# Attention on one Trainium2 core: query turned whole in pairs of heads, its high and low parts written into opposite halves of the partitions

## The reference

```
xn = layernorm(x) * g_norm
q  = xn @ Wq            # 16 heads of 64
k, v = xn @ Wkv         # one head of 64, shared by all query heads
q, k = l2norm(q) * q_scale, l2norm(k) * k_scale
p  = softmax(8 * q @ [null_k, k].T + bias)   # bias: rel_pos_bias with a causal mask, and the mask input
o  = p @ [null_v, v]
out = layernorm(o @ Wout) * g_out
```

## Time and profile before

| | us |
|---|---|
| median of 3 runs | 2564.28 |
| lowest and highest | 2559.71, 2566.23 |
| profiled execution, span | 2563.2 |
| TensorE busy, matmul | 2394.0 (93%) |
| VectorE busy | 1753.9 (68%) |
| GpSimd busy | 1333.1 (52%) |
| ScalarE busy | 1234.0 (48%) |

### The profile page before, as it was taken

The page is one execution under the profiler, slowest core; times in us unless marked ns, Lnnn a source line. Parts: engine busy times, 40 slices in busy tenths (PEclk is TensorE's granted clock), DMA queues, the critical chain, the costliest instruction groups (busy, mean ns, idle before and its releaser), DMA issues. The chain is left out here.

```text
span 2563.2 us, 56453 instructions
## 1 busy us (share of the span) xinstructions
PE 2394.0 (93%) x20705; PEld 1977.5 (77%) x20705; DVE 1753.9 (68%) x4121; ACT 1234.0 (48%) x3133; POOL 1333.1 (52%) x1464
## 2 busy tenths in 40 slices
PE   5999999999999999977999999988899999999998
PEld 3788888888888888845777777766677877778776
DVE  4576767677767676677888888337865755746764
ACT  3656666666666666554555555114333333332332
POOL 3676767676767676535666666215422322322332
PEclk8999999999999999988999999999999999999999
DMA  4000100000000000001122221216022112111211
GB/s 143 7 11 9 46 18 11 10 10 9 11 10 9 10 5 5 5 15 24 40 56 55 55 53 47 55 59 181 32 66 63 55 58 67 58 47 62 66 34 59
DMA packets 156689, 105.05 MB, mean 41 GB/s; under 512 B 85168, under 2 KB 134832, under 8 KB 156416
## 3 DMA queue, kind: packets, MB, share of 16 engines
q1 hardware_dynamic: 130928, 62.69, 9.0%
q10 hardware_dynamic: 25488, 38.73, 4.9%
HBM read 80.51 MB, written 20.88 MB: 40 GB/s over the span
## 5 line engine op out<-in xcount | busy, mean ns | idle before, releaser
L968 POOL TENSOR_TENSOR a_bm<-a_bias,a_mask_add 128x512 f32<-128x512 f32 (+3 forms) x512 | 438.4, 873 | 189.3 <-DVE a_nm L697 186.3
L1592 POOL TENSOR_TENSOR m_hid_part<-m_hid,m_hid_part 128x512 fp32r<-128x512 f32 x176 | 238.5, 1355 | 552.9 <-ACT m_hid_part L1501 547.6
L874 ACT ACTIVATE a_S<-a_S,a_nm 128x512 f32<-128x512 f32 (+3 forms) x512 | 289.3, 565 | 347.6 <-DVE a_nm L697 344.9
L697 DVE CUSTOM_DVE_ANT_0 a_S<-a_S,a_bm,a_nsn 128x512 f32<-128x512 f32 (+3 forms) x512 | 275.3, 545 | 142.1 <-PE a_S L455 137.4
L478 PE MATMUL a_O<-a_v,a_PT 128*128 128x64 f32 x2560 | 342.4, 265 | 0.0
L478 PEld LDWEIGHTS a_O<-a_v,a_PT 128*128 128x128 f32 x2560 | 328.4, 193 | 0.0
L1513 ACT ACTIVATE m_hid<-m_G 128x512 f32<-128x512 f32 x176 | 105.4, 599 | 390.9 <-PE m_G L1447 353.3
L455 PE MATMUL a_S<-a_kT,a_qT 128*128 128x384 f32 (+3 forms) x1024 | 284.0, 358 | 3.6 <-DVE a_nm L697 3.2
L1674 DVE TENSOR_TENSOR m_hid<-m_hid,m_U 128x512 f32<-128x512 f32 x176 | 121.0, 687 | 223.8 <-PE m_U L1447 190.3
L1464 PE MATMUL m_Y<-m_hid_part,m_down_high 128*128 128x512 f32 x704 | 256.5, 405 | 12.2 <-POOL m_hid_part L1592 11.4
L1447 PE MATMUL m_G<-m_in,m_gate_high 128*128 128x512 f32 x704 | 252.2, 399 | 0.9 <-POOL m_up_low L1586 0.9
(11 more groups left out here) (323 smaller groups left out, 5348.4 us busy)
## 6 DMA issues: line engine op xcount, KB each, us to landing
m_spread<-s_w ACTq DMA_DIRECT2D x64, 256.0 KB, 3.2
m_spread<-s_w ACTq DMA_DIRECT2D x128, 128.0 KB, 2.9
a_x<-in_x SPq DMA_DIRECT2D x32, 128.0 KB, 2.2
s_hT<-a_hT SPq DMA_DIRECT2D x32, 128.0 KB, 2.1
d_x<-in_x SPq DMA_DIRECT2D x8, 512.0 KB, 4.7
d_h<-s_hT SPq DMA_DIRECT2D x8, 512.0 KB, 5.2
s_xg<-d_xg SPq DMA_DIRECT2D x8, 512.0 KB, 3.1
d_x<-s_xg SPq DMA_DIRECT2D x8, 512.0 KB, 4.6
```

Source lines behind the costliest of these rows:

```text
L697: dve.tensor_tensor_reduce(S[:, n % S_SLOTS, 0:w], SB[n % 2][:, 0:w], bm[:, n % BM_SLOTS, 0:w], -1.0, nsn[:, tile % 2, h:h + 1], ALU.add, ...
L874: act.activation(S[:, n % S_SLOTS, 0:w], S[:, n % S_SLOTS, 0:w], ACT.Exp, scale=-1.0, bias=nm[:, tile % 2, h:h + 1], accum_out=den[:, tile ...
L968: pool.tensor_tensor(bm[:, n % BM_SLOTS, 0:w], bias[:, h, L - w:L], mask_add[b % 2][:, 0:w], ALU.add).then_inc(s["bm_ready"], 1)
L1592: pool.tensor_tensor(hid_part[1][:, q % H_SLOTS], hid[:, q % G_SLOTS], hid_part[0][:, q % H_SLOTS].bitcast(F32), ALU.subtract).then_inc(hi ...
```

## The change

The array `qs` and the steps qs0 and qs1 go. There are two steps qT0 and qT1 instead of four, behind heads 10 and 12, with the banks exchanged (qT0 in bank 1, qT1 in bank 0). TensorE turns the unsplit float32 query `qn`, two heads of 64 to a turn of 128x128, so 4 turns fill a bank with 8 heads. Of each pair, one head comes to lie in partitions 0 to 63 and the other in 64 to 127. For each of the two halves e, ScalarE copies the four heads in that half into the same half of `qT` (the high parts, cast to fp32r), and then VectorE subtracts these from PSUM and writes the difference (the low parts) into the other half of `qT`. So in even heads the high part lies in the lower partitions, and in odd heads in the upper ones. A step now makes four instructions, each over 64 partitions and 512 columns: two on ScalarE and, each behind one of them, two on VectorE. GpSimd's `qn` of a tile also waits until the turns of the tile before have read it.

```diff
--- before.py
+++ after.py
@@ -186,7 +186,6 @@
         rr = sb("rr", [P, NH + 1])
         qn = sb("qn", [P, NH, DH])
         kn = sb("kn", [P, 2, DH])
-        qs = sb("qs", [P, NH, 2, DH], F32R)
         qT = sb("qT", [P, 2, NH, P], F32R)
         kf = sb("kf", [P, P])
         kT = [[sb(f"kT{b}{i}", [P, L], F32R) for i in range(2)] for b in range(2)]
@@ -254,7 +253,7 @@
 
         names = ["mask_read", "bm_ready", "x_var", "x_rstd", "xn_ready",
                  "xnT_high", "xnT_low", "q_ready", "kv_ready", "sq_ready", "ss_ready", "rr_ready", "qn_ready",
-                 "q_high", "q_low", "kn_ready", "qT_act", "qT_dve", "kT_read", "kT_ready", "null_ready",
+                 "kn_ready", "qT_high", "qT_low", "kT_read", "kT_ready", "null_ready",
                  "scores_psum", "scores_ready", "probs_ready", "probsT_psum", "probsT_act", "probsT_dve", "pv_done",
                  "null_diff", "null_probs", "weights_ready", "o_scaled", "oT_act", "oT_dve", "pnrT_ready",
                  "out_var", "out_rstd", "hn_ready", "hT_ready",
@@ -269,7 +268,7 @@
 
 
         FRONT = {"stat": -5, "xn": -3, "xT": -2, "q0": 0, "q1": 1, "kv": 2, "ss": 3, "qn": 4, "kT": 7,
-                 "null": 10, "qs0": 8, "qs1": 9, "qT0": 12, "qT1": 12, "qT2": 13, "qT3": 14}
+                 "null": 10, "qT0": 10, "qT1": 12}
         BACK = {"diff1": 0, "weigh1": 4, "oT": 6, "pnT": 7, "outp": 9, "hn": 11, "hT": 13}
 
         def order():
@@ -290,14 +289,14 @@
             steps = [("mlp", 0), ("stat", 0), ("gain", 0), ("xn", 0), ("nullk", 0), ("turned", 0), ("xT", 0),
                      ("layer", 0), ("weights", 0), ("weights", 1), ("wnull", 0), ("mlp", 1), ("q0", 0), ("q1", 0),
                      ("gain", 1), ("kv", 0), ("turned", 1), ("ss", 0), ("layer", 1), ("qn", 0), ("kT", 0), ("null", 0),
-                     ("qs0", 0), ("qs1", 0), ("qT0", 0), ("qT1", 0), ("qT2", 0), ("qT3", 0),
+                     ("qT0", 0), ("qT1", 0),
                      ("narrow", 0)] + behind.get(-1, [])
             for n in range(NH * (NT + 1)):
                 steps += [("head", n)] * (n < NH * NT + PV_LAG) + behind.get(n, [])
             return steps
 
         steps = order()
-        FILLS = {"xT": 0, "q0": 1, "q1": 0, "kv": 1, "qT0": 0, "qT1": 1, "qT2": 0, "qT3": 1, "kT": 0,
+        FILLS = {"xT": 0, "q0": 1, "q1": 0, "kv": 1, "qT0": 1, "qT1": 0, "kT": 0,
                  "pnT": 1, "outp": 0, "hT": 1, "nullo": 0, "wide0": 0, "wide1": 1}
 
         filling, before, held = {}, {}, [[], []]
@@ -311,12 +310,21 @@
 
             return {"xT": [(s["xnT_low"], t + 1)], "q0": [(s["q_ready"], 2 * t + 1)],
                     "q1": [(s["q_ready"], 2 * t + 2)], "kv": [(s["kv_ready"], 3 * t + 3), (s["sq_ready"], 3 * t + 3)],
-                    "qT0": [(s["qT_act"], 2 * t + 1)], "qT1": [(s["qT_dve"], 2 * t + 1)],
-                    "qT2": [(s["qT_act"], 2 * t + 2)], "qT3": [(s["qT_dve"], 2 * t + 2)],
+                    "qT0": [(s["qT_low"], 4 * t + 2)], "qT1": [(s["qT_low"], 4 * t + 4)],
                     "kT": [(s["kT_read"], t + 1)], "oT": [((s["oT_act"], s["oT_dve"])[n], t + 1)],
                     "pnT": [(s["pnrT_ready"], t + 1)], "outp": [(s["hn_ready"], t + 1)],
                     "hT": [(s["hT_ready"], t + 1)], "nullo": [(s["null_out_ready"], 1)],
                     "wide0": [(s["wide0_ready"], t + 1)], "wide1": [(s["wide1_ready"], t + 1)]}[name]
+
+        def halves(e):
+            return slice(e * DH, e * DH + DH)
+
+        def turned_heads(t, i, e):
+
+            return qT[:, t % 2, 8 * i + e:8 * i + 8:2]
+
+        def heads_of(f):
+            return f[:, :].rearrange("p (a n) -> p a n", n=P)
 
         def evac_by_dve(n):
             return n % 4 == 3
@@ -444,8 +452,7 @@
                             w = width(n)
                             if h == 0:
 
-                                pe.wait_ge(s["qT_act"], 2 * (tile + 1))
-                                pe.wait_ge(s["qT_dve"], 2 * (tile + 1))
+                                pe.wait_ge(s["qT_low"], 4 * (tile + 1))
                                 pe.wait_ge(s["kT_ready"], tile + 1)
                             if n >= 2:
 
@@ -544,17 +551,15 @@
                             last = pe.matmul(f[:, 0:cols.stop - cols.start], xnT[i][:, k], wqkv[j][:, k, cols],
                                              start=n == 0, stop=n == len(terms) - 1)
                         last.then_inc(full[FILLS[name]], 1)
-                    elif name in ("qT0", "qT1", "qT2", "qT3"):
+                    elif name in ("qT0", "qT1"):
                         i = int(name[2])
                         if (name, t) == ("qT0", 0):
                             unread(16)
-                        if i % 2 == 0:
-                            pe.wait_ge(s["q_high"], 2 * t + 1 + i // 2)
-                            pe.wait_ge(s["q_low"], 2 * t + 1 + i // 2)
+                        pe.wait_ge(s["qn_ready"], 2 * t + 1 + i)
                         f = fill(name, t)
                         for j in range(4):
                             last = pe.transpose(f[:, j * P:(j + 1) * P],
-                                                qs[:, 4 * i + j].rearrange("p a d -> p (a d)").bitcast(F32), ident[:])
+                                                qn[:, 8 * i + 2 * j:8 * i + 2 * j + 2].rearrange("p a d -> p (a d)"), ident[:])
                         last.then_inc(full[FILLS[name]], 1)
                     elif name == "kT":
                         pe.wait_ge(s["kn_ready"], t + 1)
@@ -734,11 +739,15 @@
                             dve.wait_ge(s["rr_ready"], t)
                         link(dve.tensor_reduce(ss[:], sq[:], AX.X, ALU.add))
                         dve.tensor_scalar(ss[:], ss[:], 1e-24, None, ALU.max).then_inc(s["ss_ready"], 1)
-                    elif name in ("qT1", "qT3"):
+                    elif name in ("qT0", "qT1"):
                         f = filled(name, t)
                         i = int(name[2])
-                        dve.tensor_copy(qT[:, t % 2, 4 * i:4 * i + 4].rearrange("p a n -> p (a n)"), f[:, :])\
-                           .then_inc(s["qT_dve"], 1)
+                        for e in range(2):
+                            own, other = halves(e), halves(1 - e)
+                            dve.wait_ge(s["qT_high"], 4 * t + 2 * i + e + 1)
+                            dve.tensor_tensor(turned_heads(t, i, e)[other], heads_of(f)[own],
+                                              turned_heads(t, i, e)[own].bitcast(F32),
+                                              ALU.subtract).then_inc(s["qT_low"], 1)
                     elif name == "kT":
                         f = filled(name, t)
                         if t == 0:
@@ -906,19 +915,11 @@
                         act.copy(v[t // TT % 2][:, t % TT], f[:, DH:2 * DH]).then_inc(s["kv_ready"], 1)
                         act.copy(nraw[:], f[:, 2 * DH:2 * DH + NH]).then_inc(s["kv_ready"], 1)
                         act.copy(qraw[:, NH], f[:, 0:DH]).then_inc(s["kv_ready"], 1)
-                    elif name in ("qs0", "qs1"):
-
-                        i = int(name[2])
-                        hs = slice(8 * i, 8 * i + 8)
-                        act.wait_ge(s["qn_ready"], 2 * t + 1 + i)
-                        if t > 0:
-                            act.wait_ge(full[1], filling["qT3", t - 1, 1])
-                        act.copy(qs[:, hs, 0], qn[:, hs]).then_inc(s["q_high"], 1)
-                    elif name in ("qT0", "qT2"):
+                    elif name in ("qT0", "qT1"):
                         f = filled(name, t)
                         i = int(name[2])
-                        act.copy(qT[:, t % 2, 4 * i:4 * i + 4].rearrange("p a n -> p (a n)"), f[:, :])\
-                           .then_inc(s["qT_act"], 1)
+                        for e in range(2):
+                            act.copy(turned_heads(t, i, e)[halves(e)], heads_of(f)[halves(e)]).then_inc(s["qT_high"], 1)
                     elif name in ("diff0", "diff1"):
                         i = int(name[4])
                         n = 2 * t + 1 + i
@@ -1001,6 +1002,8 @@
                         pool.tensor_tensor(rr[:], ss[:], half[:, 0:NH + 1], ALU.pow).then_inc(s["rr_ready"], 1)
                     elif name == "qn":
                         pool.wait_ge(s["rr_ready"], t + 1)
+                        if t > 0:
+                            pool.wait_ge(full[FILLS["qT1"]], filling["qT1", t - 1, FILLS["qT1"]])
                         pool.wait_ge(s["q_ready"], 2 * (t + 1))
                         pool.wait_ge(s["kv_ready"], 3 * (t + 1))
                         if t > 0:
@@ -1012,15 +1015,6 @@
                             hs = slice(8 * i, 8 * i + 8)
                             pool.tensor_tensor(qn[:, hs], qraw[:, hs], rr[:, hs].unsqueeze(2).broadcast_to([P, 8, DH]),
                                                ALU.mult).then_inc(s["qn_ready"], 1)
-                    elif name in ("qs0", "qs1"):
-
-                        i = int(name[2])
```

(6 more changed lines are left out.)

## The result

The changed kernel takes 2753.65 us (median; 2750.3 to 2756.21) against 2564.86 us in the same comparison, a ratio of 1.0748 with a 95% interval of 1.0729 to 1.0767: 189 us slower. The forecast was slower, 2696 us, with 2750 as the upper end; the time lies 3.7 us above that end.

A forecast was written before the change was run, and what follows sets the result against it. VectorE was taken as the local bound in heads 10 to 14, though TensorE bounds the stage by shares. 2563.2 us plus 105 for waits and 28 for the clock gave 2696 us, own range 2670 to 2745, wider range 2605 to 2750.

The forecast's parts named there:

- What bounds the stage in heads 10 to 14: Attention stage: VectorE is the local bound in three widths of four, and 1.3 us from it in the fourth.
- The new waits: Heads 10 to 14: VectorE waits for ScalarE's copies, delaying TensorE 2.45 to 4.2 us a tile, 105 us in all.
- Prices: Per tile: VectorE subtractions 0.69 us each, net 1.38 us more; ScalarE half-partition copies 0.59; GpSimd 2.5 us less.
- TensorE's saved turns: Per tile, 8 fewer TensorE turns save 0.9 us, which is spent in the waits and earns nothing.
- The clock: Attention stage: TensorE's long wait before the input's turn lets its clock fall, costing 28 us; bounds 0 and 96.
- two halvings: Clock cost in the attention stage: 1.5 us a fall, half of up to 3.1, in 6 tiles of 10.
- 1 (the clock holds, 2668 us): Attention stage: waits as forecast, but the clock stays up; 2668 us (2640 to 2690), chance 0.23.
- 2 (TensorE stays the bound): Attention stage: the ScalarE to VectorE hand-over hides behind TensorE, 28 us saved; 2535 us, chance 0.09.
- 3 (only the work counts): Attention stage: VectorE's added work costs 43 us, waits cost nothing; 2606 us (2580 to 2640), chance 0.08.
- 4 (no difference): Whole kernel: the saved turns and the freed port pay just for the rest; chance 0.04.

The follow-up runs named there:

- subtractions twice: The changed kernel with each VectorE subtraction made twice, the first time into a spare tile nobody reads: 2817.84 us in a single execution.
- matmuls in the waits: The changed kernel with TensorE issuing matmuls nobody reads, 3 before the query's second turn and 9 before the input's turn: 2680.55 us, ratio 1.0467.
- wait alone: The kernel before, with VectorE's two query copies also waiting for ScalarE's copy of the same pair of steps, no added work: 2599.47 us, ratio 1.0151.
- subtractions later: The changed kernel with VectorE's subtractions moved from behind heads 10 and 12 to behind heads 11 and 13: 2671.99 us, ratio 1.0434.

## Why the prediction was right and wrong

*What bounds the stage in heads 10 to 14*: right. All of the loss is there or right behind it, and the doubled work passed through, 2.4 us a tile for 2.4 us of added instructions.

*The new waits*: right, and near in size. TensorE's waits came where they were named, 95.6 us for xn (some 90 forecast) and 56.5 for hn (some 50). Against 4.2, 3.4, 3.4 and 2.45 us, the first part of the tile grew by 4.5, 3.6, 3.4 and 2.7. Summed as there, 8 x (4.5 + 3.6 + 3.4) + 7 x 2.7 = 111 us against 105. In the tile shown, score 11 is 1.7 us later behind score 10 than in the earlier trace rows (forecast 1.6) and score 13 is 4.0 later (forecast 3.8), counted there from this row:

```profile
492.02 0.48 DVE L697 CUSTOM_DVE_ANT_0 a_S<-a_S,a_bm,a_nsn 128x256 f32<-128x256 f32 x1
```

*Prices*: right. The subtraction took 0.689 us (0.69 taken), the copy 0.577 (0.59). GpSimd's 77 us less (1256.4 for 1333.1) bought next to nothing: of VectorE's small instructions the sum L607, for which I took 0.4 us in the middle widths, took 26.2 us in the stage instead of 22.8, and the null key's L759 21.2 instead of 26.9. A pair of subtractions takes 1.41 us, and the next score starts 1.44 us after its start, so they follow each other at 0.72, not at the 0.61 of the earlier trace rows. By the rule of the Trainium skill (VectorE: DVE Perf Modes, "Two Vector instructions with no wait between them") that is what a change of halves does; the trace agrees, and the run with the subtractions twice shows the same instruction both ways, at 0.61 us without the change of halves and 0.71 with it.

*TensorE's saved turns*: right that they earn nothing here. Even placed well, in the runs made here, they were given back.

*The clock*: this is the step that failed, and by its size alone; that the new waits would let the clock fall was right. I took 28 us: a fall in 6 tiles of 10, at half of one fall's price of 3.1 us. Measured, the second part of the tile grew by 2.6, 3.0, 2.1 and 4.4 us: 8 x (2.6 + 3.0 + 2.1) + 7 x 4.4 = 92 us. That and the 111 make 203 by medians of inner tiles, against 195 in the stage. Summed over tiles 1 to 29 without medians, the second part grew by 84 us. The clock was at half for 307 us, 9.9 us a tile, in every tile and in several twice; one fall of 6.8 us was what the earlier trace rows showed, and I counted one at most. So neither of my two halvings was right: every tile paid, not 6 of 10, and it paid 2.9 to 3.0 us on average, near the full 3.1. The run with matmuls in the waits was 73 us faster and left the first part of the tile alone. The upper bound that I gave for this term, 96 us, holds it; I didn't carry it into the range, which with it would have reached 2764 us. The Trainium skill (TensorE: Matmul & The Clock Gate, "HAM oscillation — how this bites in real kernels") has a loop with a long enough stall in each turn throttled again in each turn. The trace agrees, the clock fell in every tile; the 18 us that I added by it, at 1.5 us a fall, were in the right direction and still too few.

*Rivals*: 1 (the clock holds, 2668 us) is refuted by the records of the clock; the run with matmuls in the waits, where it nearly holds, took 2680.55 us, within the 2640 to 2690 given for that case. 2 (TensorE stays the bound) is refuted by the time itself and by VectorE's 62.2 us of idle time before the subtractions. 3 (only the work counts) is refuted by the run that moves the subtractions: with the work kept and the waits gone it is 82 us faster than the changed kernel. That the work counts too, the doubled run shows. 4 (no difference) is refuted by the time.

## What to carry to other kernels

An instruction that waits for another engine's share of the same step delays what stands behind it in its own queue, and whoever needs the bank that it empties: here, moving the waiting share behind took 1.5 to 2 us a tile off the stretch, and one such wait alone, with no work, cost 39 us. So put the second share of a step a step or more behind the first, and look in the timeline, not in the averages, for the stretch where the receiving engine has room. Where a change makes TensorE wait some 3 us in every turn of a loop, count the clock in full: in every turn, and for as long as it takes to come back, but only for the time in which TensorE sets the pace.

## What the hardware showed that I had not expected

In the tile shown, a wait of 2.3 us and one of 2.9 us lie some 4 us apart, and the tile takes about 38 us. In the changed kernel the clock was at half for 307 of 1223 us. It doesn't take two waits: in tiles of width 4 the first is 0.7 us only, and with the subtractions moved later one wait of 2.5 to 2.9 us went with half clock in all 22 tiles of widths 1 to 3 between tiles 1 and 29, and one of 1.4 us at width 4 in three tiles of seven. In the kernel with the wait alone, 23 waits of 1.3 to 1.5 us left the clock up.

What half clock costs depends on who sets the pace. This is the second part of the tile, where TensorE does, summed over tiles 1 to 29 from the clock's records and the instructions' times:

| kernel | half clock in heads 10 to 14, us | half clock in the rest, us | growth of the rest over the time before, us |
|---|---|---|---|
| after | 111 | 186 | 84 |
| subtractions later | 45 | 123 | 54 |
| subtractions twice | 173 | 151 | 68 |

In all three the rest grew by 0.44 to 0.45 us per us at half clock, a little under a half, which is what work at half the clock loses. In heads 10 to 14 it cost nothing that shows: with matmuls in the waits it fell from 111 to 24 us there, and the stretch got no shorter. So the doubled run, with 348 us at half clock in the stage against 307, lost less to the clock.

And VectorE starts an instruction later when it changes the halves of the partitions: the same subtraction follows its predecessor at 0.61 us if it reads and writes the same halves, and at 0.71 us if not. Over 64 partitions it isn't faster than the groups over 128: 0.689 us for 64x512, where the copy L740 of 128x512 took 0.685, and ScalarE's copies took 0.577 us for 64x512 and 0.590 for 128x512.
